# A two-layer decoder on one core: finishing turns placed later and awaited per half, the clamp of the maxima moved to VectorE, one store later, no GpSimd drain in token stages

## The reference, cut to what matters

```python
q = (x @ wq + bq).reshape(B, SQ, N_HEADS, D_HEAD)
k = (y @ wk + bk).reshape(B, SKV, N_HEADS, D_HEAD)
v = (y @ wv + bv).reshape(B, SKV, N_HEADS, D_HEAD)
scores = jnp.einsum('bqhd,bkhd->bhqk', q, k) / jnp.sqrt(jnp.asarray(D_HEAD, x.dtype))
attn = jax.nn.softmax(scores, axis=-1)
out = jnp.einsum('bhqk,bkhd->bqhd', attn, v).reshape(B, SQ, D_EMBED)
return out @ wo + bo
```

## Time and profile before

| | |
|---|---|
| three runs | 2062.48, 2065.91, 2072.31 us; median 2065.91 |
| the profiled execution | 2067.45 us, of it 2065.7 us span from first to last instruction |
| busy share of the span | PE 90%, DVE 63%, ACT 47%, POOL 28% |
| mean granted PE clock | 0.934 of full speed |
| stages, us | at0 244.6, xa0 151.5, at1 376.4, xa1 104.9, mla 249.9; ex0 312.3, ex1 156.6; the token stages 30.9 to 88.5 |

### The profile page before, as it was taken

The page is one execution under the profiler, slowest core; times in us unless marked ns, Lnnn a source line. Parts: engine busy times, 40 slices in busy tenths (PEclk is TensorE's granted clock), DMA queues, the critical chain, the costliest instruction groups (busy, mean ns, idle before and its releaser), DMA issues. The chain is left out here.

```text
span 2065.7 us, 34219 instructions
## 1 busy us (share of the span) xinstructions
PE 1849.5 (90%) x11790; PEld 1057.6 (51%) x11791; DVE 1310.1 (63%) x2305; ACT 970.4 (47%) x1898; POOL 571.0 (28%) x955
## 2 busy tenths in 40 slices
PE   8799998777789999969999999978888999986996
PEld 4344445322689999934222222243343444465995
DVE  4588866777633333367988888455687788754113
ACT  3366663566112222243677777733423666632334
POOL 3211123333234333222011111133453111143551
PEclk9899999789689999989999999997997999987998
DMA  7634405400911111065322230064035343051224
GB/s 183 141 89 66 67 2 126 92 17 2 377 52 36 33 33 36 26 169 127 65 32 32 41 48 7 1 150 83 18 73 123 62 63 60 5 204 39 69 71 143
DMA packets 99097, 158.15 MB, mean 77 GB/s; under 512 B 31447, under 2 KB 79063, under 8 KB 93783
## 3 DMA queue, kind: packets, MB, share of 16 engines
q1 hardware_dynamic: 87122, 131.79, 27.8%
q0 software_dynamic: 7488, 20.46, 3.2%
q10 hardware_dynamic: 4352, 4.20, 0.6%
HBM read 110.67 MB, written 44.72 MB: 75 GB/s over the span
## 5 line engine op out<-in xcount | busy, mean ns | idle before, releaser
L1958 ACT ACTIVATE arena<-psum 128x512 f32<-128x512 f32 (+1 forms) x1120 | 577.0, 590 | 286.8 <-PE psum L1914 202.0
L1671 DVE TENSOR_REDUCE arena<-psum 128x1 f32<-128x1024 f32 (+7 forms) x384 | 428.8, 1156 | 83.8 <-PE psum L1629 49.3
L1914 PE MATMUL psum<-arena 99*128 99x512 bf16 (+7 forms) x1280 | 373.6, 355 | 6.4 <-ACT arena L1958 3.5
L1629 PE MATMUL psum<-arena 96*128 96x512 bf16 (+7 forms) x1280 | 355.4, 360 | 24.4 <-SPq L2668 10.6
L1932 PE MATMUL psum<-arena 128*32 128x512 f32 (+3 forms) x2560 | 280.7, 538 | 0.8 <-ACT arena L1958 0.7
L2391 PEld LDWEIGHTS psum<-arena 128*128 128x128 f32 x2340 | 275.9, 193 | 7.5 <-ACT arena L2438 3.5
L2391 PE MATMUL psum<-arena 128*128 128x128 f32 x2340 | 277.0, 276 | 2.2 <-ACT arena L2438 1.4
L2484 DVE COPY arena<-arena 128x1536 f32 (+1 forms) x117 | 97.2, 831 | 283.6 <-PE psum L2391 281.2
L1657 DVE CUSTOM_DVE_ANT_0 arena<-psum,arena 128x1024 bf16<-128x1024 f32 (+3 forms) x224 | 216.7, 1019 | 47.2 <-PE psum L1629 47.1
L1914 PEld LDWEIGHTS psum<-arena 99*128 99x128 bf16 (+1 forms) x1280 | 119.6, 99 | 236.9 <-ACT arena L1958 137.0
L1629 PEld LDWEIGHTS psum<-arena 96*128 96x128 bf16 (+1 forms) x1280 | 111.3, 100 | 181.7 <-DVE arena L1657 42.2
(11 more groups left out here) (204 smaller groups left out, 2257.9 us busy)
## 6 DMA issues: line engine op xcount, KB each, us to landing
arena<-k_parts SPq DMA_DIRECT2D x144, 128.0 KB
q_halves<-arena SPq DMA_DIRECT2D x80, 192.0 KB, 2.9
arena<-q_halves SPq DMA_DIRECT2D x40, 384.0 KB, 4.9
arena<-in_L_ffn_up SPq DMA_DIRECT2D x8, 1408.0 KB, 17.9
arena<-q_halves SPq DMA_DIRECT2D x40, 256.0 KB, 5.3
k_parts<-arena SPq DMA_DIRECT2D x48, 192.0 KB, 3.2
arena<-in_L_ffn_down SPq DMA_DIRECT2D x9, 1024.0 KB, 14.1
arena<-y_rows SPq DMA_DIRECT2D x32, 256.0 KB, 4.4
```

The lines of the kernel that those rows point to most:

```text
L1629: last = nc.tensor.matmul(dst[:, base + lo:base + hi], q[0:rows, qh, h, qb % 4 * P:qb % 4 * P + P], k[0:rows, h, key0 + lo:key0 + hi], sta ...
L1671: nc.vector.tensor_reduce(dst, src, AX.X, ALU.max).then_inc(t("taken"), 1)
L1914: last = nc.tensor.matmul(b[:, at0:at0 + width], kk[0:rows, h, kb * P:kb * P + P], q[0:rows, qh, h, c0:c1], start=True, stop=diag is None)
L1958: nc.scalar.activation(probs[k % at.ahead][:, heads[0]:heads[-1] + 1, c0:c1], bank[st_bank[no % 3]][:, 0:len(heads) * width].rearrange("p ...
```

## The change

It has five parts.

1. **OT placed later.** The planner enters an OT only when its MX has been done for 2 us by its picture (`due`), or at the latest just before the OC of the second job after it (`behind`).
2. **MX waits per half.** `pool_mix` waits for the turn of its own half `qh` of the pair of groups before (`turns_before`), not for both.
3. **Clamp moved.** The maxima are negated by the reduction itself (`negate=True`, cross-attention alone). The DVE move then clamps both ways in xa0 and is a plain copy in xa1; POOL's clamp instruction is gone. The planner's costs follow (`MixQueue` 1.9 for both, landing 4.0 instead of 3.5).
4. **One store later.** In at0 and at1 SP issues the 1 MB store of the context values (`early_sp`) after the maxima load of job 1, not ahead of it.
5. **No POOL drain** in any token stage. Where POOL adds to `x_tok` it waits for its own last addition instead.

```diff
@@ class MixQueue
+    def due(self, time):
+        return bool(self.turns) and self.turns[0][0] + 2.0 <= time
+
+    def behind(self, j):
+        return bool(self.turns) and self.turns[0][1] < j
@@ plan(), in both attention classes
+        def turn_next():
+            mixed, j = queue.turns.pop(0)
+            self.events.append(("OT", j))
+            on_dve(mixed, 0.72)
         def turn_until(time):
             queue.mix_until(time)
-            while queue.turns and queue.turns[0][0] <= max(free["DVE"], time):
-                mixed, j = queue.turns.pop(0)
-                self.events.append(("OT", j))
-                on_dve(mixed, 0.72)
+            while queue.due(max(free["DVE"], time)):
+                turn_next()
...
                     queue.mix_until(float("inf"))
+                    while queue.behind(j - 1):
+                        turn_next()
                     self.events.append(("OC", j))
@@ CrossAttention.plan
-        moves, queue = [], MixQueue(self.events, 2.5 if self.clip else 1.75)
+        moves, queue = [], MixQueue(self.events, 1.9)
-                landed[j] = queue.split(taken[-1]) + 3.5
+                landed[j] = queue.split(taken[-1]) + 4.0
@@ token_stage
+                if any(kind == "more" for kind, n in plan.get("POOL", [])):
+                    pool.wait_ge(t("pool_x"), n_pairs)
-            if source == "comb":
-                progs["undrained"] = "pool"
+            progs["undrained"] = "pool"
@@ CrossMaxima
-                nc.vector.tensor_reduce(dst, src, AX.X, ALU.max).then_inc(t("taken"), 1)
+                nc.vector.tensor_reduce(dst, src, AX.X, ALU.max, negate=True).then_inc(t("taken"), 1)
-                    nc.vector.tensor_scalar(m_f2[j % 2][0:32, :], self.region(turn)[0:32, 0:P], -1.0, -CLAMP / QSCALE,
-                                            ALU.mult, ALU.max).then_inc(t("taken"), 1)
+                    nc.vector.tensor_scalar(m_f2[j % 2][0:32, :], self.region(turn)[0:32, 0:P], CLAMP / QSCALE,
+                                            -CLAMP / QSCALE, ALU.min, ALU.max).then_inc(t("taken"), 1)
-                if at.clip:
-                    nc.gpsimd.tensor_scalar(m[0:32, :], m[0:32, :], CLAMP / QSCALE, None, ALU.min)\
-                        .then_inc(t("m_step"), 1)
@@ Outputs
+            def turns_before(self, j):
+                g, qh = self.at.jobs[j]
+                if g < 2:
+                    return 0
+                last = 2 * (g // 2) - 1
+                return 2 * (g // 2 - 1) + [q for n, q in self.at.jobs if n == last].index(qh) + 1
-                wait(pool, t("turned"), 2 * (g // 2))
+                wait(pool, t("turned"), self.turns_before(j))
@@ self_attention_stage, sp_prog
-                if early_sp:
-                    early_sp(sp)
...
                     maxima.load(sp, 2 * g + 1)
+                    if g == 0 and early_sp:
+                        early_sp(sp)
```

More of the change, by code:

```diff
@@ L1753, in dve_move @@
                 if at.clip:
-                    nc.vector.tensor_scalar(m_f2[j % 2][0:32, :], self.region(turn)[0:32, 0:P], -1.0, -CLAMP / QSCALE,
-                                            ALU.mult, ALU.max).then_inc(t("taken"), 1)
+                    nc.vector.tensor_scalar(m_f2[j % 2][0:32, :], self.region(turn)[0:32, 0:P], CLAMP / QSCALE,
+                                            -CLAMP / QSCALE, ALU.min, ALU.max).then_inc(t("taken"), 1)
                 else:
-                    nc.vector.tensor_scalar(m_f2[j % 2][0:32, :], self.region(turn)[0:32, 0:P], -1.0, None, ALU.mult)\
+                    nc.vector.tensor_copy(m_f2[j % 2][0:32, :], self.region(turn)[0:32, 0:P])\
                         .then_inc(t("taken"), 1)
@@ L1763, in pool_split @@
                 pool.wait_ge(t("taken"), at.turn["MT", j] + 1)
-                steps = 4 if at.clip else 3
-                done = steps * j
-                if at.clip:
-                    nc.gpsimd.tensor_scalar(m[0:32, :], m[0:32, :], CLAMP / QSCALE, None, ALU.min)\
-                        .then_inc(t("m_step"), 1)
-                    done += 1
-                    pool.wait_ge(t("m_step"), done)
+                done = 3 * j
                 wait(pool, t(f"mld{j % 2}"), 48 * (j // 2))
```

## The result

The changed kernel takes 2045.4 us (median of 4 runs, 2041.9 to 2048.4) against 2065.5 us before on the same chip: ratio 0.9893, 95% interval 0.9872 to 0.9914. 2044 was predicted, from a stage-by-stage sum. The profiled execution has a span of 2042.9 us, 22.8 less than before.

| stage | before, us | after, us | difference | predicted |
|---|---|---|---|---|
| at0 | 244.6 | 242.5 | -2.1 | 0 |
| t1 | 45.7 | 43.4 | -2.3 | -0.5 |
| xa0 | 151.5 | 141.8 | -9.7 | -12.8 |
| at1 | 376.4 | 378.0 | +1.6 | 0 |
| t4 | 45.9 | 44.9 | -1.0 | 0 |

The account below looks back on a forecast made before the run. PE's own work bounds at0, at1 and mla; in xa0 PE waits for DVE, which waits for POOL's mixes. -12.8 - 4.4 - 1.0 - 3.9 - 0.5 = -22.6 us from 2067.45 gave 2044.9, stated as 2044; range 2033 to 2056.

Parts of the forecast that it names:

- Turns and mixes, xa0: In xa0, turns later and mixes earlier remove six PE waits behind DVE's waits for POOL's mix: -16.7 us.
- The rule for turns as the cause: In xa0, DVE's 13.9 us of waits for POOL at the turns fall to 1 us or less, removing PE's waits.
- Collisions: In xa0, POOL work now beside clips: one mutual hold-up of 0.29 us charged per turn, eight turns, +2.4 us.
- The third rival: The shared port takes it back: 7 us return in xa0, not 2.4, hitting clips; total -18.0 us; chance 0.07.
- the sign "mean well over 0.72 us": In xa0, the prediction is wrong if the clips' mean duration rises well over 0.72 us.
- Late maxima: In xa0, fewer matmuls before the scores needing the maxima; 0.5 us each for jobs 5, 10 and 13, +1.5 us.
- xa1: In xa1, two PE waits of the same kind go, -4.4 us, and waits for maxima to land shrink, -1.0 us.
- Drain: At the end of t4, without POOL's drain PE starts with SP's, at the head of xa1: -3.9 us.
- the second rival: At the end of t4, the POOL stall stays under another name, the rest as summed: -18.7 us, 2048.7; chance 0.10.
- Clamp, negation: POOL's clamp leaves t1's chain, -0.5 us; in xa0 it is within other terms; negation in the reduction assumed free.
- Store: In at0 and at1, the later store is covered by slack ahead of what needs the first mix: price 0.
- Self-attention: In at0, at1 and mla, new lists with nearly the same distances and the same matmuls: price 0, bounds +4 and -2.

Follow-up runs that it names:

- no_drain: The kernel before with no POOL drain in any token stage, nothing else changed: 2062.1 us, ratio 0.9979.
- bias_beside_reduce: Changed kernel with the old self-attention plans, and xa0's 16 POOL bias additions each held until DVE starts a reduction: 2037.6 us, ratio 0.9851 to the kernel before.
- landing_cost_5: bias_beside_reduce with the planner's cost for the maxima to land at 5.0 us instead of 4.0: 2037.5 us, ratio 0.9862 to the kernel before.

## Why the prediction was right

The order of cross-attention brought most of the gain and the drain some 4 us, as said. That the sum came within 2 us is in part luck: terms that were too large and too small cancelled. The parts measured alone multiply to 0.9919 x 0.9979 x 0.9974 x 1.0013 x 1.000 = 0.9885, within the interval of the whole (0.9872 to 0.9914). Against the steps of the prediction:

- **Turns and mixes, xa0 (-16.7).** The six long waits are gone, as named. That this was worth -16.7 was too simple: with DVE 86% busy (122.6 of 141.8 us), shorter waits for DVE stand in other places, and PE's listed waits for DVE fell only from 21.0 to 17.7 us. All of PE's idle time in xa0 fell by 4.6 us only. The other 5.1 us of the stage are less PE time for the same matmuls, at a clock of 0.87 and not 0.85. The prediction saw that the clock "points the same way" and gave it no term.
- **The rule for turns as the cause.** The prediction ties the gain to POOL being ahead of DVE at the turns. In this order that is so; but two other orders gained the same with that wait half there. The old order was the cause, the rule one of several ways out of it.
- **Collisions (+2.4).** Mis-sized: 5.8 us on DVE (7.4 us of the stage went when the bias additions did), since I took 0.29 us, from a pair of short instructions, for each of eight turns. One collision costs a clip up to 1.05 us, when a bias addition and a mix stand back to back, and 14 clips took over 0.8 us. The third rival was in this right in kind and nearer in size (7 us); the sign "mean well over 0.72 us" came true at 0.786, and the stage took 141.8 us and not about 139. The time still came out, since other terms were too small.
- **Late maxima (+1.5).** 3.6 us, at three jobs as said, but not at jobs 5, 10 and 13: at 4, 6 and 15. The jobs were picked from a wrong count. The 53 and 40 matmuls for job 5 are instructions of the list, but the rate of 139 in 20.5 us counts the profile's records, and the profile has two for each matmul of the values in fp32. In records the distance went from 58 to 49, which is 7.2 us at that rate and not 5.9, and 49 (jobs 5, 10 and 13) is the longest in the stage, not the shortest: jobs 4, 6 and 15 have 46, 43 and 30. That three jobs wait all the same is luck. For job 4 the move was at 393.5 us and the last part landed at 399.8, 6.3 us and not 5, because the split runs beside clips (its first cast takes 0.60 us in the mean, where it took 0.35).
- **xa1 (-5.4).** -8.7 in these two profiles. Waits for reductions fell 3.3 us and those for loads 3.1, a new one for OC took 2.8 back, and PE's busy time fell 4.9 us with the clock, as low as in no_drain with the old order (83.0 us). All six kernels with this order had xa1 at 95.2 to 96.2 us without its head, the five with the old one 101.7 to 108.8: the nearest two are 5.5 us apart, the farthest 13.6.
- **Drain (-3.9).** Right to 0.1 us; the second rival is out.
- **Clamp, negation (-0.5 in t1, nothing else of its own).** t1 was 43.8 us in the mean of seven traces with the clamp moved (42.8 to 45.2) and 45.0 in seven without (44.0 to 45.8): shorter, but its size is not to be told from such scatter. In xa0 it is worth 4.1 us with the old order.
- **Store (0).** Right. But it landed in 5.4 us and not 11.3, and the first mix moved 3.2 us later in the stage and not 9.
- **Self-attention (0).** Wrong by 1.5 us in at1; the prediction had looked at distances, waits and the number of matmuls. Its cause is open: PE's waits are the same (2.0 us for ACT), the loss grows over the jobs (0.8 us by the third, 1.6 at the end), and the changes from one kind of matmul to another are fewer in the new order (641), not more (671). at0 and mla moved by 2 us, one down and one up, and not within 1 us as said; t6 and ex1 moved as much though no edit changes their plan, and together took 190.3 us before and 190.0 after.

## What to carry to other kernels

Before a gain is put down to a planner's new rule, have it draw once more with nothing but a cost changed: here three other orders were all 0.8 to 1% faster than the one before. A wait that is removed on a full engine mostly comes back elsewhere; what stays is read from busy time and clock as well as from waits, and over several traces, since the clock of one execution can hide or feign 5 us in a stage. Count matmuls in one unit, either instructions or records of the profile. And place POOL's larger SBUF work beside VectorE's reductions out of PSUM, not beside its instructions with two SBUF inputs.

## What had not been expected of the hardware

- A clip that starts behind a POOL addition waits for the next one as well, if that follows without a gap: 1.73 us for an instruction of 0.68, three times in xa0 of the changed kernel.
- POOL's drain at the end of t4 took 7.94 us in each of the seven kernels that have it, with four different plans of cross-attention among them.
- The same stretch of work in xa0 costs PE 117.9, 112.8 or 108.8 us of busy time at a mean clock of 0.85, 0.87 and 0.90 (before, changed, bias_beside_reduce). It went down together with PE's waits in these three, but 118.7 us at 0.84 with as few waits as in the last of them (landing_cost_5) shows that waits alone don't decide it.
